# Turning the normalised rows by DMA instead of on TensorE in a cross-attention and feed-forward kernel

## What is computed

```python
x = x + xattn(layernorm(x), ctx, ctx, mask, w_q, w_k, w_v, w_o)   # 16 heads, 64 wide
w = quantize_int4(kernel)
h = layernorm(x)
x = x + h @ w + bias + (h @ a) @ b
```

## Time and profile before

| | us |
|---|---|
| median of 3 runs | 540.42 (539.54 to 540.65) |
| the profiled execution | 538.71 |
| its span, first to last instruction | 536.9 |
| PE busy | 468.2 (87%) |
| DVE busy | 423.2 (79%) |
| POOL busy | 400.3 (75%) |
| ACT busy | 330.9 (62%) |
| queue of the DMA transposes, share of 16 DMA engines | 64.9% |

### The profile page before, as it was taken

One profiled execution on the slowest core, in us unless ns is written; L12 is line 12 of the kernel. 1 busy time (PEld: TensorE's weight loads), 2 busy tenths in 40 slices (PEclk: granted clock), 3 DMA queues, 4 the chain that ended last, 5 costly groups with the idle time before them and its releaser, 6 DMA issues.

```text
span 536.9 us, 15609 instructions
## 1 busy us (share of the span) xinstructions
PE 468.2 (87%) x5939; PEld 337.9 (63%) x5939; DVE 423.2 (79%) x1138; ACT 330.9 (62%) x839; POOL 400.3 (75%) x658
## 2 busy tenths in 40 slices
PE   2239678998999899999999899989999999988874
PEld 0125365667766686667766776668666777666663
DVE  4945757988898888988898879888798878888762
ACT  4815456676667776676567666776667656666521
POOL 3364187888878787879878887878787787789941
PEclk9559979999999999999999999999999999999897
DMA  8310157668866788688767896688757786679950
GB/s 304 109 59 21 29 132 146 112 127 165 159 120 123 135 186 123 125 149 165 141 112 136 160 160 123 125 129 189 130 120 149 97 146 130 131 130 168 178 130 24
DMA packets 217953, 71.10 MB, mean 132 GB/s; under 512 B 202497, under 2 KB 216594, under 8 KB 217874
## 3 DMA queue, kind: packets, MB, share of 16 engines
q1 hardware_dynamic: 216528, 67.65, 64.9%
q0 software_dynamic: 768, 2.10, 1.2%
q10 hardware_dynamic: 578, 0.30, 0.2%
HBM read 15.50 MB, written 4.19 MB: 37 GB/s over the span
## 4 chain that ended last, share of the span: by engine, by line
PE 48%; DVE 27%; ACT 13%; POOL 5%; issue 4%; DMA 2%; POOLq 0%; DVEq 0%; ACTq 0%
PE ps_b L812 38%; DVE ps_a L703 6%; PE ps_a L874 6%; ACT arena L586 6%; DVE arena L696 4%; ACT arena L577 2%; PE ps_b L915 2%; DVE arena L652 2%; PE ps_b L891 2%; DVE arena L775 1%; DVE arena L707 1%; POOL arena L512 1%; DMA mask_u<-in_mask_1x1xSxS_bk_dram 1%; POOL arena L516 1%; ACT arena L593 1%
## 5 line engine op out<-in xcount | busy, mean ns | idle before, releaser
L812 PE MATMUL ps_b<-arena 128*128 128x65 f16 (+3 forms) x3456 | 346.3, 253 | 14.6 <-DVE arena L676 5.3
L812 PEld LDWEIGHTS ps_b<-arena 128*128 128x128 f16 x3456 | 234.2, 99 | 103.1 <-DVE arena L676 6.7
L586 ACT ACTIVATE arena<-ps_a,arena 128x160 f32<-128x160 f32 x512 | 159.4, 395 | 95.9 <-DVE arena L707 87.5
L516 POOL TENSOR_TENSOR arena<-arena 128x512 f16<-128x512 f32 x128 | 148.2, 1158 | 0.0
L512 POOL CAST arena<-arena 128x512 f16<-128x512 f32 x128 | 78.2, 611 | 74.7 <-ACT arena L586 74.7
L703 DVE TENSOR_REDUCE ps_a<-ps_a 128x4 f32<-128x640 f32 x128 | 105.4, 823 | 0.2
L874 PE MATMUL ps_a<-arena 64*128 64x160 f16 x1536 | 76.4, 233 | 14.5 <-ACT arena L586 11.2
L874 PEld LDWEIGHTS ps_a<-arena 64*128 64x128 f16 x1536 | 50.9, 95 | 39.2 <-issue 22.2
L891 PE MATMUL ps_b<-arena 128*128 128x65 f16 x512 | 71.7, 194 | 0.0
L696 DVE TENSOR_TENSOR arena<-ps_b,arena 128x512 f16<-128x512 f32 x64 | 43.7, 686 | 24.9 <-ACT arena L577 24.1
L775 DVE TENSOR_TENSOR arena<-ps_b,arena 128x256 f32<-128x256 f32 x128 | 54.3, 425 | 4.4
(11 more groups left out here) (122 smaller groups left out, 437.5 us busy)
## 6 DMA issues: line engine op xcount, KB each, us to landing
arena<-in_x_dram SPq DMA_DIRECT2D x8, 512.0 KB, 5.2
mask_u<-in_x_dram SPq DMA_DIRECT2D x32, 128.0 KB, 2.9
out_dram<-mask_u SPq DMA_DIRECT2D x32, 128.0 KB, 2.4
arena<-arena SPq DMA_TRANSPOSE x128, 3.8
arena<-in_L_xattn_w_k_dram SPq DMA_DIRECT2D x1, 1024.0 KB, 8.5
arena<-in_L_xattn_w_v_dram SPq DMA_DIRECT2D x1, 1024.0 KB, 10.5
arena<-in_L_xattn_w_q_dram SPq DMA_DIRECT2D x1, 1024.0 KB, 12.3
arena<-in_L_xattn_w_o_dram SPq DMA_DIRECT2D x1, 1024.0 KB, 14.2
```

The lines of the kernel that those rows point to most:

```text
L516: nc.gpsimd.tensor_tensor(lo_main, main, hi_main, ALU.subtract)
L586: ins = nc.scalar.activation(probs[k % 2][:, h, :], p_scores[k % 2][:, h % 2, h // 2 * WINDOW:(h // 2 + 1) * WINDOW], ACT.Exp, bias=neg_ma ...
L812: mm = nc.tensor.matmul(dst, a, c, start=(first and at == 0), stop=(last and at == n - 1))
```

## The change

The normalised input of batches 1 to 7 and the second norm's result are no longer turned by TensorE. ACT writes each norm's result twice from the same source, once as float32 and once rounded to float16 (the high half). POOL subtracts the two and writes the low half. SP turns both halves with one DMA transpose of four blocks of 128 by 128. The items `x0`, `x1` are left in the start alone, for batch 0; item `n` is gone with its work on PE, ACT and DVE. `q` waits for `x_turned`, `f` for `x2_turned`. In the diff below, the pieces after the lists are SP's, POOL's (`x_low` and the subtraction of `x2`), ACT's, DVE's (`w`) and PE's (`q` and the late items), in this order. `x_low` stands behind `split_probs` in the slots in which SP has `turn_x`.

```diff
-        PROJ = [["c", "x0"], ["x1"], ["k0"], ["k1", "k2"],
+        PROJ = [["c"], [], ["k0"], ["k1", "k2"],
-        LATE = [[("n", 3)], [("w", 2)], [("f", 3), ("o0", 1)], [("o1", 1)]]
+        LATE = [[], [("w", 2)], [("f", 3), ("o0", 1)], [("o1", 1)]]
...
+            def turn_x(t, batch):
+                sp.wait_ge(x_lo_made, ST * (batch - 1) + t + 1)
+                if batch == 1:
+                    sp.wait_ge(item_made, ALL_PROJ.index("q7") + 1)
+                else:
+                    u = next(u for u in range(NS) if "q7" in PROJ[u])
+                    sp.wait_ge(item_made, items_at[(batch - 2) * NS + u] + PROJ[u].index("q7") + 1)
+                sp.dma_start_transpose(
+                    xT[:, :, :, t * P:(t + 1) * P].rearrange("p i d q -> p (i d) q"),
+                    x_half[t].rearrange("p i d -> p (i d)")).then_inc(x_turned, 16)
+            def turn_x2(tile):
+                sp.wait_ge(x2_lo_made, tile + 1)
+                if tile >= 1:
+                    k = (tile - 1 + 3) * NG + 2
+                    proj, late = slot_items(k)
+                    sp.wait_ge(item_made, items_at[k] + len(proj) + late.index(("f", tile - 1)) + 1)
+                sp.dma_start_transpose(x2T.rearrange("p i d q -> p (i d) q"),
+                                       x2_half.rearrange("p i d -> p (i d)")).then_inc(x2_turned, 16)
             def slot(s):
                 if s.k < LAST:
                     turn_probs(s.k)
+                if s.k == 0:
+                    for t in range(ST):
+                        turn_x(t, 1)
+                if s.u > NS - ST and s.norm_ahead:
+                    turn_x(s.u - (NS - ST) - 1, s.batch + 2)
+                if s.u == 0 and 1 <= s.batch < B - 1:
+                    turn_x(ST - 1, s.batch + 1)
+                tile = s.k // NG - 3
+                if s.g == 0 and 0 <= tile:
+                    turn_x2(tile)
...
+            def x_low(t, batch):
+                pool.wait_ge(xn_made, ST * batch + t + 1)
+                nc.gpsimd.tensor_tensor(x_half[t][:, 1], xn[:, t, :], x_half[t][:, 0], ALU.subtract) \
+                    .then_inc(x_lo_made, 1)
...
+                if s.g == 0 and 0 <= tile:
+                    pool.wait_ge(x2_made, tile + 1)
+                    nc.gpsimd.tensor_tensor(x2_half[:, 1], x2, x2_half[:, 0], ALU.subtract).then_inc(x2_lo_made, 1)
...
             def norm_apply(t, n):
                 act.wait_ge(ln_rstd_made, n)
+                if n >= 3:
+                    act.wait_ge(x_turned, 16 * ST * (n - 2))
                 nc.scalar.activation(xn[:, t, :], x_in[:, t, :], ACT.Identity, bias=ln_shift[:, t:t + 1],
+                                     scale=ln_rstd[:, t:t + 1])
+                nc.scalar.activation(x_half[t][:, 0], x_in[:, t, :], ACT.Identity, bias=ln_shift[:, t:t + 1],
                                      scale=ln_rstd[:, t:t + 1]).then_inc(xn_made, 1)
...
-                        nc.scalar.activation(x2, x1, ACT.Identity, bias=t_shift[:, :], scale=t_rstd[:, :]) \
-                            .then_inc(x2_made, 1)
+                    nc.scalar.activation(x2, x1, ACT.Identity, bias=t_shift[:, :], scale=t_rstd[:, :])
+                    nc.scalar.activation(x2_half[:, 0], x1, ACT.Identity, bias=t_shift[:, :], scale=t_rstd[:, :]) \
+                        .then_inc(x2_made, 1)
...
                 elif name == "w":
+                        dve.wait_ge(x2_made, tile)
...
                 elif kind == "q":
+                    if s.k >= 0:
+                        pe.wait_ge(x_turned, 16 * ST * (s.batch + 1))
...
-                elif name == "n":
-                    pe.wait_ge(x2_made, tile + 1)
-                    for d in range(DT):
-                        mm = nc.tensor.transpose(bank[:, d * P:(d + 1) * P], x2[:, d * P:(d + 1) * P], ident[:, :])
                 else:
-                    pe.wait_ge(item_done, items_at[s.k - 1])
+                    pe.wait_ge(x2_turned, 16 * (tile + 1))
```

43 lines of the change are left out of this document (26 added, 17 removed).

## The result

The changed kernel takes 545.38 us at the median (542.48 to 546.65, 7 runs) where the kernel before takes 539.54 us beside it: 1.0107 times as long, 95% interval 1.0073 to 1.0141. It is slower, by 1.1%; the forecast was 534.6 us. The profiled execution takes 544.33 us, its span is 542.5 us (before 538.71 and 536.9).

The account below looks back on a forecast made before the run. PE was taken to bound the middle and POOL the last batch. Batches -11.3, start +1.0, last batch +2.4 and drain +2.1 sum to -5.8 us, so 540.42 becomes 534.6 us; eight-in-ten range 526 to 545.

Parts of the forecast that it names:

- The start, +1.0: Start of the run: four more ACT instructions cost 2.0 us, some 1.0 comes back in slots 0 and 1; +1.0 us.
- ACT's chain at the boundary: Batch boundary: two activations more delay the exponentials, PE waits 2.5 us, so each of six boundaries gains 0.90 us, not 3.42.
- `n` in the other slots: 19 slots with g = 0 outside boundaries, before the last batch: dropping `n` gains 0.31 us each, 5.9 us.
- The DMAs, "at nothing": SP's 60 transposes, a third the size, cost nothing; `f` at the boundary has 6.2 us for its transpose and one ahead.
- The gap at its own length only: Slot 1 of a boundary: PE's wait for the late exponentials counted as 2.5 us of time and nothing more.
- POOL's low halves: Eight subtractions a batch on POOL, 0.62 us each, 5.0 us in all, covered by its gaps and so put at nothing.
- rival (b): POOL becomes the bound at the boundary if a subtraction costs near 1.16 us; slower, 547.6 us; chance 0.22.
- The last batch, +2.4: Last batch, bound by POOL: three subtractions cost 1.9 us and ACT's second activation 0.5; +2.4 us, between 1.3 and 4.6.
- The drain, +2.1: Last tile: second norm to `f` takes 4.6 us in place of 2.44; +2.1 us, between 1.7 and 3.1.
- Rival (c): Turned rows come late: at 1309 ns a block `f` waits 4.3 us at each of six boundaries; 560 us; chance 0.03.

Follow-up runs that it names:

- x_only: Changed kernel with only the input's part kept, the second norm's result turned by PE as in the kernel before; 531.40 us, 0.9863 of the kernel before.
- after_again: The changed kernel timed once more, with no edit; 545.07 us, 1.0131 of the kernel before.
- tail_pe: Changed kernel with the second norm's result of the last seven tiles turned by PE as in the kernel before; 539.22 us, 1.0031 of that kernel.
- act_gather: Changed kernel with norm_apply moved to slots 12 to 14 and the context gather and load of x to slot 3; 541.45 us.
- x_only_ae: Changed kernel with only the input's part kept and norm_apply moved to slots 12 to 14; 526.10 us, 0.9757 of the kernel before.
- act_swap_tail: Changed kernel with norm_apply in slots 12 to 14, x2's transpose ahead of x's, and the last seven tiles' second norm turned by PE; 531.32 us.
- x2_early: Changed kernel with x2, its low half and its turn made a slot earlier, behind the exponentials; 550.58 us, 1.0202 of the kernel before.
- q_early: Changed kernel with norm_apply in slots 12 to 14 and the input's tiles turned in slots 13 to 15; 549.6 us.
- swap: Changed kernel with x2's low half and transpose put ahead of those of the input's last tile in a batch's first slot; 544.51 us.

## Why the prediction was wrong, point by point

**The start, +1.0:** it is 0.55 us from slot 3 on, and 0.33 at slot 16, behind `n`'s gain in slot 12.

**ACT's chain at the boundary:** right. PE waits 2.42 us (2.5 forecast), the two slots gain 0.92 (0.90), the chain goes L649, L651, L679, L680, L640. An undisturbed batch lasts 294.64 - 237.96 = 56.68 us (56.5).

**`n` in the other slots:** 0.23 us each, not 0.31. I took the whole distance from its start to the next scores; the slots got shorter by less (slot 12 by 0.22, slots 28 and 44 by 0.27): 4.4 us in place of 5.9.

**The DMAs, "at nothing":** this step failed, and with it the forecast. The budget was right: low half to `f` 131.00 - 124.73 = 6.27 us, 6.2 forecast. What had to fit was not. I took 3.8 us for a landing and one transpose ahead of it, and priced that by its size. SP needs as long to issue four blocks as twelve, and there were two ahead; then the landing took 5.06 us at that boundary and 3.4 to 4.4 at four of the others. In the trace of the kernel after:

```profile
L462 SPq DMA_TRANSPOSE arena<-arena x128: 1275/1451/3242, 60.6 to 518.1; - x128
```

```profile
L485 SPq DMA_TRANSPOSE arena<-arena x32: 1201/1526/2207, 111.3 to 533.8; - x32
```

(ns on the queue: least, median, most.) 2.83 + 5.06 = 7.9 us. I also wrote that nothing counts behind SP's waiting instruction; what counted was what stood ahead of x2's.

**The gap at its own length only:** I priced 2.5 us of an idle PE as 2.5 us. The trace of before has no such gap in the middle, and in it a granted clock of 0.94 in the last batch, where PE waits for exponentials, was the sign to follow. Three falls cost 3.8 us; with `f`'s waits it is 7.4. With `n`'s 1.5, the start's -0.45 and the boundaries' -0.1 that makes 8.3, all that lies between the -10.3 us that I forecast at slot 112 and the -2.0 that the trace has there.

**POOL's low halves:** 670 ns each, at the line through the two that I had put a little lower:

```profile
L584 POOL TENSOR_TENSOR arena<-arena x32: 662/668/678, 109.7 to 533.1; 128x256 f16<-128x256 f32 x32
```

In 210 to 270 us POOL is busy for 55.42 us, 92%, as forecast, and its waits for exponentials fall from 8.5 to 2.4:

```profile
POOL arena L550 <- ACT arena L640: 2.4, 5, 1.0
```

In the middle no exponentials wait for POOL, so rival (b) is not what happened, though its number, 547.6, is the nearest. That it has the right sign is luck: x_only keeps four of the eight low halves of a batch and is 7.2 us faster than before.

**The last batch, +2.4:** it is +4.38, near the upper bound. Slot 113 costs 1.63 (the clock: in after_again, without a fall, it lasts 3.73 us as before), slot 118 1.55 (`f` for its transpose), slot 121 1.59 (the clock), and three slots give 0.86 back. Slot 112 costs 0.49, ACT's second activation, as forecast. So in this trace the 1.9 us of POOL's low halves are not what the slots that grew wait for. POOL's chain did get longer (the longest wait of the exponentials for it is 1.78 us, before 1.15), and what it would cost if `f` didn't wait no run shows: tail_pe takes both away.

**The drain, +2.1:** +3.19. The last tile has 5.07 us in place of 4.6 (the transpose 3.07 from its issue, 2.8 forecast), +2.63; the rest is in the tiles before it, where SP issues x2's turn behind the last probabilities and a store (518.14, 519.48, then 520.57, with the low half there at 518.7).

**Rival (c),** 0.03, is the one whose mechanism came true, at two boundaries in place of six and for another reason: SP's order and a late landing. The Trainium skill, "VectorE: DVE Perf Modes", section "The three transpose paths", gives 1309 ns for a block, by which an estimate for four is 5.2 us, and the 5.06 us above looks like it. But four blocks land in 3.07 us in the drain, and in act_gather in 2.4 us at the least and 3.3 at the median, and twelve in 3.9 at the median; so it isn't a price per block here. The 5.06 us go with a DMA share of 1.31 (below); that load alone makes the difference is argued, not shown. The Trainium skill, "VectorE: DVE Perf Modes", section "Rules for kernel authors", advises TensorE for a 128 by 128 transpose where its result may go to PSUM; that holds here for the second norm (x_only_ae 526.1 against act_swap_tail 531.3 us) and not for the input (x_only 7.2 us faster than before).

**What stays open:** how load and `f`'s own waits share the second norm's loss in the middle; why equal gaps of 2.42 us have a fall behind them in some boundaries and not in others; why the drain of x2_early is 2.7 us longer than that of the kernel after; and what POOL's low halves alone cost in the last batch.

## What to carry to other kernels

A DMA transpose held its queue here for about 1.5 us, with four blocks as with twelve: count transposes, not bytes, list what stands ahead of the urgent one in program order, and issue the one with the nearest deadline first. When a fix gives nothing, look what took its place before dropping it: here shortening the gap and mending the order gave 0.5 us each and 8.3 together. Move work to another engine where its result has slots of slack (the input, used four slots later), and leave it where it has two or fewer (the second norm, above all in the tail, where nothing else covers it).

## What the hardware showed that I had not expected

- SP holds the queue for 1451 ns at the median for a transpose of twelve 128x128 blocks and 1526 for four; the least is 1275 and 1201.
- Four blocks land in 3.07 us in the drain and in 5.06 us at a boundary, with a DMA share of 1.31 from 128 to 132 us (packets are counted where they start, so it can be above 1); in q_early it took 6.9 us. Twelve blocks: 3.7 us at the least, 3.9 at the median, 7.0 at the most.
- Behind an idle PE of 2.42 us its granted clock was 0.50 for over a microsecond in three boundaries of six, in after_again in two, in swap and tail_pe in five; behind 1.45 us in the middle it was in none, though behind 1.42 us in the last batch (slot 121) it was. It costs 1.2 to 1.7 us each time.
